# A feature-interaction tower: sums over d moved ahead of the spread group's product, another order of the front, and chunk 0's layer 0 by single tiles

## The reference, cut to what matters

```
e = stack([tbl_f[ids[:, f]] for f in range(39)], axis=1)              # (512, 39, 16)
z0 = einsum('bid,bjd->bdij', e, e).reshape(B, D, 39 * 39)
cur0 = relu(einsum('bdk,kl->bld', z0, W0))                           # 128 maps
next_h, direct0 = split(cur0, 2, axis=1)                             # 64 and 64
z1 = einsum('bid,bjd->bdij', e, next_h).reshape(B, D, 39 * 64)
cur1 = relu(einsum('bdk,kl->bld', z1, W1))                           # 128 maps
z = sum(concatenate([direct0, cur1], axis=1), axis=-1)               # over d
h = concatenate([z, dense_ctx], axis=1)
y = relu(relu(h @ W_top1 + b_top1) @ W_top2 + b_top2) @ W_top3
```

## Time and profile before

| | |
|---|---|
| timed runs | 438.61, 439.88 (median), 444.40 us |
| profiled execution | 437.52 us |
| its span | 435.7 us, 4074 instructions |
| granted TensorE clock, mean | 0.978 |
| PE busy | 400.6 us (92%) |
| DVE busy | 345.7 us (79%) |
| POOL busy | 294.6 us (68%) |
| ACT busy | 226.0 us (52%) |
| moved by DMA | 80.80 MB, 185 GB/s over the span |

### The profile page before, as it was taken

One profiled execution on the slowest core, in us unless ns is written; L12 is line 12 of the kernel. 1 busy time (PEld: TensorE's weight loads), 2 busy tenths in 40 slices (PEclk: granted clock), 3 DMA queues, 4 the chain that ended last, 5 costly groups with the idle time before them and its releaser, 6 DMA issues.

```text
span 435.7 us, 4074 instructions
## 1 busy us (share of the span) xinstructions
PE 400.6 (92%) x1426; PEld 249.0 (57%) x1426; DVE 345.7 (79%) x196; ACT 226.0 (52%) x224; POOL 294.6 (68%) x164
## 2 busy tenths in 40 slices
PE   0868977999999899999999799999999999997897
PEld 0734634666666546666656356565656565664464
DVE  0305748799999798999998788999999989999800
ACT  3025544474738356564746273847475656553422
POOL 3778889888888888888888888898989800000000
PEclk9989998999999989999999799999999999999999
DMA  8384956496969497878879493959886888992000
GB/s 309 81 218 128 260 135 176 123 247 187 242 165 265 120 262 178 232 199 216 210 214 222 138 281 78 290 137 233 195 253 187 219 218 226 261 253 56 2 0 0
DMA packets 27862, 80.80 MB, mean 185 GB/s; under 512 B 7265, under 2 KB 16225, under 8 KB 20034
## 3 DMA queue, kind: packets, MB, share of 16 engines
q1 hardware_dynamic: 22146, 77.64, 65.9%
q0 software_dynamic: 5120, 1.32, 3.3%
q10 hardware_dynamic: 576, 1.58, 1.1%
HBM read 76.58 MB, written 3.93 MB: 185 GB/s over the span
## 4 chain that ended last, share of the span: by engine, by line
POOL 44%; PE 39%; issue 9%; DMA 3%; DVE 3%; ACT 0%; DVEq 0%
POOL found L277 44%; PE acc L499 7%; PE acc L531 6%; PE acc L524 5%; PE acc L523 5%; PE acc L542 5%; PE sums L482 3%; DMA found<-in_table_dram,rows_sb 2%; PE acc L538 2%; DVE z_lo L418 2%; PE spread L571 2%; DMA ids_sb<-in_ids_dram 1%; PE spread L512 1%; DVE z L410 1%; PE sums L560 1%
## 5 line engine op out<-in xcount | busy, mean ns | idle before, releaser
L277 POOL DMA_INDIRECT found<-in_table_dram,rows_sb x160 | 294.4, 1840 | 53.6 <-issue 48.5
L320 ACT ACTIVATE z_hi<-z 128x2048 fp32r<-128x2048 f32 x64 | 122.4, 1912 | 95.5 <-DVE z L410 95.5
L418 DVE TENSOR_TENSOR z_lo<-z,z_hi 128x2048 fp32r<-128x2048 f32 x64 | 145.8, 2279 | 0.0
L410 DVE TENSOR_TENSOR z<-x_wide,h 128x2048 f32<-128x2048 f32 x64 | 144.8, 2281 | 0.0
L499 PE MATMUL acc<-squares,w 128*128 128x512 f32 (+1 forms) x224 | 110.8, 612 | 0.0
L523 PE MATMUL acc<-z_hi,w_hi 128*128 128x512 f32 x256 | 107.3, 419 | 0.7 <-ACT cur L313 0.7
L524 PE MATMUL acc<-z_hi,w_lo 128*128 128x512 f32 x256 | 101.0, 394 | 0.0
L531 PE MATMUL acc<-z_lo,w_hi 128*128 128x512 f32 x256 | 84.3, 452 | 10.7 <-DVE z_lo L418 10.7
L296 ACT ACTIVATE squares<-sums 128x1024 f32<-128x1024 f32 x64 | 58.4, 913 | 35.5 <-PE sums L482 35.5
L531 PEld LDWEIGHTS acc<-z_lo,w_hi 128*128 128x128 f32 x256 | 47.9, 190 | 36.4 <-issue 15.2
L499 PEld LDWEIGHTS acc<-squares,w 128*128 128x128 f32 (+1 forms) x224 | 41.8, 192 | 28.8 <-issue 24.6
(11 more groups left out here) (44 smaller groups left out, 134.0 us busy)
## 6 DMA issues: line engine op xcount, KB each, us to landing
x_wide<-x_rows SPq DMA_DIRECT2D x64, 512.0 KB, 8.1
x_wide<-x_rows SPq DMA_DIRECT2D x112, 256.0 KB, 9.9
x_parts<-x_rows SPq DMA_DIRECT2D x32, 128.0 KB, 2.6
x_rows<-found SPq DMA_DIRECT2D x16, 240.0 KB, 2.2
x_wide<-x_rows SPq DMA_DIRECT2D x16, 192.0 KB, 7.2
found<-in_table_dram,rows_sb POOLq DMA_INDIRECT x160, 7.6
w_sb<-in_w_dram SPq DMA_DIRECT2D x1, 1280.0 KB, 8.1
x_wide<-x_rows SPq DMA_DIRECT2D x16, 64.0 KB, 6.7
```

The costliest lines, as they stand in the source:

```text
L277: pool.indirect_dma_start(out=found[:, b, 2, s * D:s * D + D], out_offset=None, in_=table, in_offset=bass.IndirectOffsetOnAxis(ap=rows_sb[ ...
L320: nc.scalar.activation(z_hi[:, n % RING], z[:, n % RING], ACT.Copy).then_inc(hi_done, 1)
L410: nc.vector.tensor_tensor(z[:, n % RING], x, h[:, c % 2, :].unsqueeze(1).to_broadcast([P, QUADS, N]), ALU.mult).then_inc(multiplied, 1)
L418: nc.vector.tensor_tensor(z_lo[:, n % RING], z[:, n % RING], z_hi[:, n % RING], ALU.subtract).then_inc(lo_done, 1)
```

## The change

It touches three things.

1. **DVE's loop.** `reduce0(c + 1)` and `reduce1(c - 1)` go ahead of `multiply(n + 1)` in group 4, which is the spread group's product of the next chunk. `split(c + 2)` goes from group 0 to group 1, on ACT and on DVE. The first reductions are placed by hand (n = 2 and n = 6).
2. **The front.** ACT issues its transfers only when the ids are in; w0 goes to SP's queue ahead of w1; the top layers' weights are loaded behind chunk 1's transfers. Chunk 0's row numbers get an addition of their own. `place` becomes a function of a queue and a half: in chunk 0 the second half is issued by ACT. `keep_busy` issues 21 products instead of 30, after chunk 0's gathers. In chunks 0 and 1 a square goes ahead of `evict1`, and `split(2)` on ACT ahead of `high_part(3)`.
3. **Chunk 0's layer 0** goes tile by tile: `add_up_tile`, `square_tile`, `contract0_tile`. The semaphores of layer 0 count tiles instead of duos (`tiles0`). The first product of layer 1 and its copy are made in two halves.

The diff, cut to its core:

```diff
@@ sync
+            def place(queue, c, half): ...
-                place(c)
+                place(sp, c, 0)
+
+                if c:
+                    place(sp, c, 1)
             sp.dma_start(ids_sb[:, :, :], ids).then_inc(ids_in, 16)
+            sp.dma_start(w0[:, :, :], w0a).then_inc(w0_in, 16)
+            sp.dma_start(w0b_sb, w0b).then_inc(w0_in, 16)
             sp.dma_start(w1_sb[:, :, :], w1).then_inc(w1_in, 16)
-            for dst, src in ((wt1a_sb[:, :], wt1[HALF:HALF + P, :]),
...
             widen(1, 2)
             widen(1, 3)
+            for dst, src in ((wt1a_sb[:, :], wt1[HALF:HALF + P, :]),
...
@@ gpsimd
-            pool.wait_ge(rows_ready, 1)
             for c in range(CHUNKS):
                 b = c % BUFS
+                if c < 2:
+                    pool.wait_ge(rows_ready, c + 1)
@@ scalar
+            def square_tile(t):
+
+                rows = slice(0, P) if t < T0 - 1 else slice(HALF, P)
+                act.wait_ge(summed, t + 1)
+                if t >= 2 * RING0:
+                    act.wait_ge(contracted0, t - 2 * RING0 + 1)
+                nc.scalar.activation(squares[rows, t // 2 % RING0, t % 2, :], sums[rows, t % 2, :],
+                                     ACT.Square).then_inc(squared, 1)
...
+            act.wait_ge(ids_in, 16)
             act.dma_start(select_in, select).then_inc(select_in_done, 16)
-            act.dma_start(w0[:, :, :], w0a).then_inc(w0_in, 16)
-            act.dma_start(w0b_sb, w0b).then_inc(w0_in, 16)
             act.dma_start(mix_sb[:, :, :], mix).then_inc(mix_in, 16)
...
             split(0)
-            for d in range(ND):
-                square(d)
+            place(act, 0, 1)
+            for t in range(T0):
+                square_tile(t)
             split(1)
             evict0(0)
-            high_part(0)
+            act.wait_ge(half_multiplied, 1)
+            nc.scalar.activation(z_hi[:, 0, 0:2], z[:, 0, 0:2], ACT.Copy).then_inc(half_hi_done, 1)
+            act.wait_ge(multiplied, 1)
+            nc.scalar.activation(z_hi[:, 0, 2:], z[:, 0, 2:], ACT.Copy).then_inc(hi_done, 1)
             for c in range(CHUNKS):
                 for g in range(G):
                     n = G * c + g
+                    if g == 0 and c < 2:
+                        square(ND * (c + 1))
                     if g == 0 and c:
                         evict1(c - 1)
-                    if g == 0 and c < 2:
-                        square(ND * (c + 1))
...
-                    if g == (2 if c else 3) and c + 1 < CHUNKS:
+                    if g == 2 and c + 1 < CHUNKS:
                         evict0(c + 1)
-                    if n == 2:
-                        split(2)
-                    if g == 0 and 0 < c < CHUNKS - 2:
+                    if g == 1 and c + 2 < CHUNKS:
                         split(c + 2)
@@ vector
-            nc.vector.tensor_tensor(rows_sb[:, :, :], ids_sb[:, 1:, :],
-                                    ids_sb[:, 0:1, :].to_broadcast([P, CHUNKS, SLOTS]), ALU.add).then_inc(rows_ready, 1)
+            nc.vector.tensor_tensor(rows_sb[:, 0, :], ids_sb[:, 1, :], ids_sb[:, 0, :], ALU.add).then_inc(rows_ready, 1)
+            nc.vector.tensor_tensor(rows_sb[:, 1:, :], ids_sb[:, 2:, :],
+                                    ids_sb[:, 0:1, :].to_broadcast([P, CHUNKS - 1, SLOTS]),
+                                    ALU.add).then_inc(rows_ready, 1)
...
                     n = G * c + g
-                    if n == 3:
-                        split(2)
+
+                    if g == G - 1 and 0 < c < CHUNKS - 1:
+                        reduce0(c + 1)
+                        reduce1(c - 1)
                     if n + 1 < G * CHUNKS:
                         multiply(n + 1)
-                    if g == G - 1 and c + 1 < CHUNKS:
-
-                        reduce0(c + 1)
-                        if c:
-                            reduce1(c - 1)
                     if is_v(n):
                         low_part(n)
-                    if n == 0:
+                    if n == 2:
                         reduce0(0)
-                    if g == 0 and 0 < c < CHUNKS - 2:
+                        split(2)
+                    if n == G + 1:
+                        reduce0(1)
+                    if g == 1 and 0 < c < CHUNKS - 2:
                         split(c + 2)
@@ tensor
+            def contract0_tile(t):
+                pe.wait_ge(squared, t + 1)
+                rows = slice(0, P) if t < T0 - 1 else slice(HALF, P)
+                nc.tensor.matmul(acc0[:, :], w0[rows, t, :], squares[rows, t // 2 % RING0, t % 2, :],
+                                 start=(t == 0), stop=(t == T0 - 1)).then_inc(contracted0, 1)
...
-            keep_busy(acc0, 30)
-            add_up(0)
+
+            pe.wait_ge(found_hi_done, 1)
+            keep_busy(acc0, 21)
+            add_up_tile(0)
+            add_up_tile(1)
             spread_out(0)
             pe.wait_ge(w0_ready, 2)
-            for d in range(ND):
-                if d + 1 < ND:
-                    add_up(d + 1)
-                contract0(d)
+            for t in range(T0):
+                if t + 2 < T0:
+                    add_up_tile(t + 2)
+                contract0_tile(t)
```

More of the change, by code:

```diff
@@ L56, with tiles0 @@
 BUFS = 3
+def tiles0(q):
+    return q // ND * T0 + q % ND * 2
 def is_v(n):
@@ L170, in build @@
         multiplied = sem("multiplied")
+        half_multiplied = sem("half_multiplied")
         hi_done = sem("hi_done")
+        half_hi_done = sem("half_hi_done")
         lo_done = sem("lo_done")
@@ L187, in uses, with place @@
             return c // BUFS + 1
+        def place(queue, c, half):
+            b = c % BUFS
+            queue.wait_ge(rows_out[b], 16 * uses(c))
+            start = x_rows[b, half, 0, 0:1]
+            queue.dma_start(x_parts[half:P:2, b, :].bitcast(F32),
+                            bass.AP(start.tensor, start.offset, [[N, 2 * STEP], [STEP * N, QUADS], [1, N]])
+                            ).then_inc(placed[b], 16)
         block = ctx.enter_context(nc.Block())
@@ L199, in lay_out @@
                              found[:, b, :, :]).then_inc(rows_out[b], 16)
-            def place(c):
-                b = c % BUFS
-                sp.wait_ge(rows_out[b], 16 * uses(c))
-                for half in range(2):
-                    start = x_rows[b, half, 0, 0:1]
-                    sp.dma_start(x_parts[half:P:2, b, :].bitcast(F32),
-                                 bass.AP(start.tensor, start.offset, [[N, 2 * STEP], [STEP * N, QUADS], [1, N]])
-                                 ).then_inc(placed[b], 16)
             def widen(c, i):
@@ L292, in square @@
                 rows = slice(0, P) if n == 2 else slice(HALF, P)
-                act.wait_ge(summed, q + 1)
+                act.wait_ge(summed, tiles0(q + 1))
                 if q >= RING0:
-                    act.wait_ge(contracted0, q - RING0 + 1)
-                nc.scalar.activation(squares[rows, q % RING0, 0:n, :], sums[rows, 0:n, :], ACT.Square).then_inc(squared, 1)
+                    act.wait_ge(contracted0, tiles0(q - RING0 + 1))
+                nc.scalar.activation(squares[rows, q % RING0, 0:n, :], sums[rows, 0:n, :], ACT.Square).then_inc(squared, n)
+            def square_tile(t):
[5 more added lines that the diff above has]
+                                     ACT.Square).then_inc(squared, 1)
             def evict0(c):
                 par = c % 2
-                act.wait_ge(contracted0, ND * (c + 1))
+                act.wait_ge(contracted0, T0 * (c + 1))
                 if c >= 2:
@@ L448, in _ @@
             split(1)
-            multiply(0)
+            dve.wait_ge(h_ready, 2)
+            dve.wait_ge(spread_done, 1)
+            nc.vector.tensor_tensor(z[:, 0, 0:2], spread[:, 0:2, :],
+                                    h[:, 0, :].unsqueeze(1).to_broadcast([P, 2, N]), ALU.mult).then_inc(half_multiplied, 1)
+            nc.vector.tensor_tensor(z[:, 0, 2:], spread[:, 2:, :],
+                                    h[:, 0, :].unsqueeze(1).to_broadcast([P, 2, N]), ALU.mult).then_inc(multiplied, 1)
             for c in range(CHUNKS):
@@ L483, in add_up, with add_up_tile @@
                                             start=True, stop=True)
-                last.then_inc(summed, 1)
+                last.then_inc(summed, len(DUOS[q % ND]))
+            def add_up_tile(t):
+                if t == 0:
+                    pe.wait_ge(placed[0], 32)
+                if t >= 2:
+                    pe.wait_ge(squared, t - 1)
+                nc.tensor.matmul(sums[:, t % 2, :], select_sb[:, t, :], x_parts[:, 0, :],
+                                 start=True, stop=True).then_inc(summed, 1)
+            def contract0_tile(t):
[3 more added lines that the diff above has]
+                                 start=(t == 0), stop=(t == T0 - 1)).then_inc(contracted0, 1)
             def keep_busy(acc, count):
@@ L500, in contract0 @@
```

(2 more changed lines are left out.)

29 lines of the change are left out of this document (15 added, 14 removed).

## The result

| | before | after |
|---|---|---|
| timed runs, us | 438.61, 439.88, 444.40, 446.64 | 420.11, 422.05, 423.91, 435.25 |
| median, us | 442.14 | 422.98 |
| profiled execution, its span | 437.52, 435.7 | 420.11, 418.3 |
| granted TensorE clock, mean | 0.978 | 0.994 |
| PE, DVE, POOL, ACT busy, us | 400.6, 345.7, 294.6, 226.0 | 393.4, 346.1, 260.1, 227.9 |

The ratio of after to before is 0.957, 95% interval 0.944 to 0.970. The forecast was 420.5 us with a range of 414 to 431, and for the span 417.6 against 418.3 found, in the fastest of the four runs (the spans of the others are 420.2, 422.1 and 433.4). Medians here take in all runs of a kernel, but ratios and intervals leave out those over 1.5% above its fastest (435.25 and 446.64 here), and loop_only and high_first, with two such runs of four each, have no interval.

What follows compares the result with a forecast made beforehand. PE's own work, 22.25 us per undisturbed chunk, was taken as the bound, plus 9.8 us lost to late gathers. Span 435.7 - 2.1 - 5.3 - 9.8 - 0.9 = 417.6, 419.4 with 1.8 around it, forecast 420.5, range 414 to 431.

Steps and rivals of the forecast that it cites:

- up to chunk 1's x_parts: Front: chunk 1's x_parts, at which PE starts again, move from 42.12 to 40.0, -2.1 us.
- to chunk 1's first high product: Front, from PE's restart: earlier split(2) and moved square make the stretch 29.7 us instead of 35.0, -5.3 us.
- later chunks: Chunks after the front: POOL no longer falls behind, so the time lost to late gathers goes, -9.8 us.
- last chunk: End of the run: DVE ends last there and is 0.9 us ahead, -0.9 us.
- Ids: Start: ids land at 3.6 us instead of 4.97, with 2.9 and 4.97 as bounds.
- Chunk 0's first sums: Front: chunk 0's x_parts land about 2.1 us earlier, near 24, a gain largely hidden by split(1).
- Steady chunks: DVE's 0.94 us wait leaves split, about 1.0 us idle precedes z_lo, and POOL passes eleven gathers per period against ten needed.
- row 160.11: DVE timeline before the change: a 0.59 us pause before the spread product; that chunk's gather of 164.38 took 2.30 us.
- Rival (c): DVE's loop: lost gathers starve until DVE pauses, +3.4 us a chunk, +44 over 13 chunks, 464.5 us; chance 0.06.
- the two readings: Port rule on DVE and POOL: a gather waits for one instruction's end, or an unbroken DVE row always comes first.
- Rival (a): Steady chunks: gathers stay at nine, the 9.8 us remain while the front gain stays, 430.3 us; chance 0.18.
- Later split: Steady chunks: wide transfers start 2.6 us later and may make DVE wait; cost 0, bound 0.5 us a chunk.

Runs made afterwards that it cites:

- loop_only: Kernel before with only the loop's two edits, from chunk 1 on: sums ahead of the spread product, split one product later; 434.82 us, no interval.
- high_first: Kernel after with PE's first high product of chunk 0 (eight matmuls) ahead of chunk 1's first sums; 429.06 us, no interval.
- duos: Kernel after with chunk 0's layer 0 computed two tiles at a time again; 423.99 us, 0.958 of before.
- sums_behind: Kernel after with the sums over d behind the spread group's product again, split still one product later; 422.93 us, 0.957 of before.
- eleven_gathers: Kernel after with an eleventh gather per chunk from chunk 3 on, into an unread buffer; 450.34 us on a chip where ACT stood still in the front.
- front_only: Kernel after with both loop edits undone, only the front's edits left; 436.35 us, 0.984 of before.

## Why the prediction was right, by its steps

| term | forecast | found |
|---|---|---|
| up to chunk 1's x_parts | -2.1 | -0.97 (42.12 to 41.15) |
| to chunk 1's first high product | -5.3 | -6.18 (77.16 to 70.01 less the row above) |
| later chunks | -9.8 | -9.05 |
| last chunk | -0.9 | -1.2 |
| span | 417.6 | 418.3 |

The third row is worked out as the rest: 17.4 in all less 7.15 in the front and 1.2 in the end. For the last row, the spread product of chunk 15 comes 16.2 us earlier (388.90 to 372.69) and the end 17.4. The first two rows miss by 1.1 and 0.9 in opposite directions, so that their sum, 7.15 of 7.4, is closer than either: partly luck.

**Ids.** Right in kind, better than taken: 2.80 instead of 3.6, ahead even of the lower bound of 2.9. POOL's first gather starts at 3.25.

**Chunk 1's x_parts, mis-sized by half.** The data for PE's restart came 0.97 us earlier and not 2.1. Split(1) was taken at 33.4 and came at 34.37, 1.12 us earlier than in the earlier trace rows though the ids came 2.17 us earlier. POOL's first gather comes 2.33 us earlier, the last of chunk 1 only 1.55 (30.92 to 29.37), as the forecast took it; DVE's addition of w0 (5.85, two SBUF inputs) held one of chunk 0's gathers to 1.87 us on the way, where the forecast had said "its gathers keep their pace". The rest is the landing: the forecast let it gain 0.6 us from wide transfers that start earlier, but split(1) came 5.00 us after that gather's start, where it had been 4.57.

**Chunk 0's first sums, wrong but hidden.** They were taken near 24 and came at 26.01. The 21 keep-busy products took 7.93 us, behind a pause of PE of 3.16; in duos the same 21 took 5.09 behind a pause of 1.18. As the cover of split(1) held, the 2 us cost nothing.

**From there to chunk 1's high product, right.** Gather 29 went through in 1.90 us (43.94), split(2) came at 54.22 (forecast 54.3), the spread product at 59.65 (59.4), the high product at 70.01 (69.4 to 70). What bound split(2) in the end was PE's sums ahead of it in ACT's order and no gather.

**Steady chunks: the outcome right, its reason half wrong.** The step that DVE's pause leaves split for the free stretch and POOL then passes eleven holds to the gather, and the deficit costs 9 to 10 us. The reason given, "I take the win, since DVE's pause is the common trait", is half shown: its row 160.11 had the pause ahead of the spread product, as sums_behind has it, and with a pause in the stretch 73 of 76 requests won. But the pause moves the request as well, and the runs don't tell the two apart. What failed is the credit: the change's first item, the sums ahead of the product, has no effect that shows (422.93 us without it, 422.98 with it, on two chips), and the forecast had let it share the gain. Rival (c)'s condition, "if a lost gather stays out until DVE pauses", is what all long gathers show; its 44 us were not paid, since in the kernel after only one request was lost.

Beside this, from the Trainium skill, page "SBUF — State Buffer", section "Who interferes with whom": of its rule that whoever issues first holds the port pair for the whole instruction (the section says it of VectorE's two-port modes), the two readings weighed in the forecast are each borne out by other rows. The request of 108.71 waits for one instruction (2.55 us), and the one of 18.42 us in eleven_gathers waits out an unbroken row of them.

**Rival (a), about rightly priced.** It said that with nine gathers the 9.8 us remain "while the front gain stays", 430.3, or 0.978 of the median it started from. The kernel with just that, front_only, measured 0.984, and its interval (0.973 to 0.994) holds 0.978. Its trace would price it higher, as its loop took 4.3 us more than before's, but that is one execution of each.

**Later split.** Cost 0 held in the kernel after: DVE waited 1.8 us in all for x_wide, three times, 0.91 at most. It is no fixed zero: duos waited 7.0 us in ten times and took 270.14 us for chunks 2 to 14, loop_only 6.4 us in seven and 271.06, against the 268.02 of the kernel after. That these waits cost the difference isn't shown. Waits of the kernel after:

```profile
DVE z_lo L441 <- ACT z_hi L341: 11.7, 14, 1.1
DVE z L433 <- DMA x_wide<-x_rows: 1.8, 3, 0.9
```

## What to carry to other kernels

Where an engine with slack stands between a producer and PE, ask not how long its pause is but where it lies: here 0.94 us moved on DVE, by moving split two instructions, lets POOL pass eleven gathers instead of nine, which was worth more than the whole front. Change one edit at a time before crediting any: of the loop's two, one gave the steady gain. And check that whatever feeds the steady part keeps the pace of an earlier start, else the next wait can take some of it back.

## What the runs showed of the hardware that was not expected

A gather issued from 0.29 us before to 0.33 us into a z_lo that follows the spread product or the sums, with no pause of DVE in the stretch, nearly always loses not one DVE instruction but all up to DVE's next pause or sums over d: 7.18 to 7.79 us where that is the pause in front of split, 14.02 (duos) and 18.42 us (loop_only, eleven_gathers) where DVE ran through. With a pause of 0.80 us or more in the stretch and a request 0.38 to 0.6 us into that z_lo, 54 of 54 waited for one instruction only (2.67 us and less). In every one of the 77 long cases the gather ended 0.8 to 0.9 us after DVE stopped or began its sums.

PE's granted clock in the kernel after, by stretch:

```profile
38.00:41.15 3.15, 0.19 (x2) 0.03 (x1) 3.15 (x3) 1.44 (x2) 2.72 (x2) 1.00 0.74 190
41.15:45.00 3.85, 3.85 (x10) 3.07 (x11) 3.85 (x2) 2.82 (x2) 3.24 (x3) 0.56 0.99 266
45.00:70.00 25.00, 24.76 (x87) 14.64 (x86) 20.17 (x12) 13.88 (x15) 20.73 (x15) 1.00 0.89 218
```

After 3 us nearly without work PE ran 3.85 us at a mean of 0.56 (1.2 GHz for most of it), and its high products stood 0.43 us apart instead of 0.23. In the kernel before, behind a wait of 1.71 us at the same place, they stood 0.23 apart at once (from 42.66). Eight of them cost 1.6 us so (8 x 0.20), a cost of the pause that the forecast had not counted and that its 29.7 us for the stretch had room for (28.86 found).
